# Twelve units in the row rings of two graph convolutions, and twelve early tiles of x1, in a graph network kernel on one core

## What is computed

```python
h = jnp.maximum(_layernorm(x, axis=-1), 0.0)
x = x + _L0_gnn_ref(h, src, dst, ...)          # attention, 8 heads; the sum is called x1
h = jnp.maximum(_layernorm(x, axis=-1), 0.0)
x = x + _L1_gnn_ref(h, edge_index, W1, b1, W2, b2)

def _gcn_layer(x, W, b, src, dst, n_nodes):    # twice, each with a relu behind it
    h = x @ W
    deg = segment_sum(ones, dst) + 2.0
    dinv = rsqrt(deg)
    msgs = h[src] * (dinv[src] * dinv[dst])[:, None]
    return segment_sum(msgs, dst) + h * (2.0 * dinv * dinv)[:, None] + b
```

## Time and profile before

| | us |
|---|---|
| median of three runs | 5014.36 |
| the profiled execution, as timed | 5055.62 |
| its span, first to last instruction | 5053.7 |
| TensorE matmul busy | 3857.4 (76%) |
| GpSimd busy | 2442.9 (48%) |
| VectorE busy | 2345.6 (46%) |
| ScalarE busy | 2192.1 (43%) |
| DMA | 803.60 MB, mean 159 GB/s |

### The profile page before, as it was taken

The page is one execution under the profiler, slowest core; times in us unless marked ns, Lnnn a source line. Parts: engine busy times, 40 slices in busy tenths (PEclk is TensorE's granted clock), DMA queues, the critical chain, the costliest instruction groups (busy, mean ns, idle before and its releaser), DMA issues.

```text
span 5053.7 us, 77590 instructions
## 1 busy us (share of the span) xinstructions
PE 3857.4 (76%) x18550; PEld 2260.5 (45%) x18551; DVE 2345.6 (46%) x4398; ACT 2192.1 (43%) x5340; POOL 2442.9 (48%) x2548
## 2 busy tenths in 40 slices
PE   4579998666777677779777777778897777777777
PEld 3369983455555555554323323333343333233333
DVE  5268887456666566678322222222353222222226
ACT  3245541344444444445444444444443444444444
POOL 3510001455555555543466666666503666666666
PEclk8789999788888888889888888899898888888899
DMA  6522225555555555555566665566514666656668
GB/s 246 156 56 59 82 62 167 159 154 160 157 163 156 143 149 149 147 150 199 182 177 174 176 177 169 167 174 176 159 68 147 180 176 179 172 166 170 174 173 309
DMA packets 317266, 803.60 MB, mean 159 GB/s; under 512 B 67665, under 2 KB 97251, under 8 KB 316241
## 3 DMA queue, kind: packets, MB, share of 16 engines
q0 software_dynamic: 193760, 629.95, 43.6%
q1 hardware_dynamic: 94981, 120.30, 7.5%
q10 hardware_dynamic: 28428, 52.40, 3.0%
HBM read 718.21 MB, written 85.04 MB: 159 GB/s over the span
## 4 chain that ended last, share of the span: by engine, by line
PE 56%; another core or an unknown queue 18%; issue 11%; ACT 6%; DVE 4%; ACTq 2%; DMA 1%; SPq 1%; DVEq 1%; POOL 0%; POOLq 0%
PE mm L1661 13%; PE tr L1661 12%; PE mm L1490 7%; PE mm L1582 4%; PE mm L1638 4%; PE tr L1582 4%; PE sm L1638 4%; ACT eler_hots L1391 3%; ACT eler_hots L1382 2%; PE tr L1638 2%; PE hist_ps L1638 2%; PE sm L1527 1%; PE tr L1485 1%; DVE big L854 1%
## 5 line engine op out<-in xcount | busy, mean ns | idle before, releaser
L1249 POOL DMA_INDIRECT edge<-h_tab,src_group x1564 | 1493.6, 955 | 1098.5 <-issue 425.2
L1391 ACT ACTIVATE eler_hots<-eler_hots,ones 128x256 f32<-128x256 f32 x1320 | 663.6, 503 | 1192.6 <-remote 632.0
L1661 PE MATMUL tr<-edge,eler_hots 128*128 x1760 | 932.6, 673 | 304.9 <-DVE big L854 130.5
L1661 PE MATMUL mm<-edge,eler_hots 128*128 x1760 | 918.4, 667 | 290.1 <-ACT eler_hots L1391 173.2
L1249 POOL DMA_INDIRECT rows_wmat<-v_tab,src_group x782 | 741.3, 948 | 601.2 <-DVE edge L828 363.0
L1382 ACT ACTIVATE eler_hots<-iota,ndrel 128x128 f32<-128x128 f32 x2640 | 915.9, 394 | 178.6 <-issue 15.6
L1661 PEld LDWEIGHTS mm<-edge,eler_hots 128*128 128x128 f32 x1760 | 371.0, 216 | 823.5 <-issue 817.5
L854 DVE TENSOR_TENSOR big<-big,mm 128x512 f32 x440 | 302.6, 688 | 935.5 <-remote 391.3
L1661 PEld LDWEIGHTS tr<-edge,eler_hots 128*128 128x128 f32 x1760 | 365.0, 213 | 828.1 <-issue 828.0
L854 DVE TENSOR_TENSOR big<-big,tr 128x512 f32 x440 | 302.6, 688 | 806.4 <-remote 334.9
L1638 PE MATMUL mm<-edge,eler_hots 128*128 128x260 f32 x1176 | 419.5, 442 | 272.8 <-ACT eler_hots L1391 176.1
(11 more groups left out here) (231 smaller groups left out, 3897.2 us busy)
## 6 DMA issues: line engine op xcount, KB each, us to landing
h_tab<-rows_wmat SPq DMA_DIRECT2D x98, 256.0 KB, 2.0
edge<-h_tab,src_group POOLq DMA_INDIRECT x1564
rows_wmat<-low_tab SPq DMA_DIRECT2D x191, 128.0 KB
ht_tab<-rows_wmat SPq DMA_DIRECT2D x49, 256.0 KB
big<-ht_tab ACTq DMA_DIRECT2D x49, 256.0 KB
v_tab<-rows_wmat ACTq DMA_DIRECT2D x49, 256.0 KB
x_tab<-big SPq DMA_DIRECT2D x49, 256.0 KB, 2.1
rows_wmat<-v_tab,src_group POOLq DMA_INDIRECT x782
```

The lines of the kernel that those rows point to most:

```text
L1249: pool.indirect_dma_start(ring[:, 2 * u + c, :], None, tab, bass.IndirectOffsetOnAxis(ap=src_group[:, n:n + 1], axis=0)).then_inc(a["rows_ ...
L1391: act.activation(onehot[:, s.j % 2, :, :], dist[:, :, :], ACT.Relu, bias=ones[:, 0:1], scale=-1.0).then_inc(a["onehot_set"], 1)
L1661: last = pe.matmul(sum_ps[bank][:, :], onehot[:, s.j % 2, n, :], edge[:, ds(slot[0][s.j] + n * D, D)], start=(n == 0), stop=(n == 1))
```

## The change

The ring of the graph convolutions has 12 units, 24 slots, and takes nearly all of `edge`. The eight tiles of x1 that lay behind the ring have no place there; EARLY_X1 is 12, all in the row and weight buffers, loaded where twelve were loaded before. ScalarE's loads behind the stores so are 37, not 29, and each is issued 12 tiles and not 20 ahead of its tile. 12 is no power of two, so the slot of a step is computed in the way of the ring of 6.

```diff
-RING = (6, 8)
-SIXTH = -(-2 ** 16 // 6)
+RING = (6, 12)
+PARTS = [-(-2 ** 16 // units) for units in RING]
...
-EARLY_X1 = 20
+EARLY_X1 = 12
...
-        early_x1 = edge[:, 2 * RING[1] * D:2 * RING[1] * D + 8 * D].rearrange("p (s n) -> p s n", n=D)
...
-            return early_x1[:, t, :] if t < 8 else rows[:, t - 8, :] if t < 16 else wmat[:, t - 16, 0:D]
+            return rows[:, t, :] if t < SLOTS else wmat[:, t - SLOTS, 0:D]
...
-            did(dve.tensor_scalar(slotcol_i[0][:, :], gidx[:, :], float(SIXTH), None, ALU.mult))
-            did(dve.tensor_scalar(slotcol_i[0][:, :], slotcol_i[0][:, :], 16, None, ALU.arith_shift_right))
-            did(dve.tensor_copy(cols[:, 4, :], slotcol_i[0][:, :]))
-            did(dve.scalar_tensor_tensor(cols[:, 5, :], cols[:, 4, :], -float(RING[0]), cols[:, 0, :], ALU.mult, ALU.add))
-            did(dve.tensor_scalar(slotcol_i[0][:, :], cols[:, 5, :], -1.0, float(2 * AW), ALU.add, ALU.mult))
-            did(dve.tensor_scalar(slotcol_i[1][:, :], gidx[:, :], RING[1] - 1, None, ALU.bitwise_and))
-            did(dve.tensor_scalar(slotcol_i[1][:, :], slotcol_i[1][:, :], float(2 * D), None, ALU.mult))
+            for slotcol, units, part, width in zip(slotcol_i, RING, PARTS, (AW, D)):
+                did(dve.tensor_scalar(slotcol[:, :], gidx[:, :], float(part), None, ALU.mult))
+                did(dve.tensor_scalar(slotcol[:, :], slotcol[:, :], 16, None, ALU.arith_shift_right))
+                did(dve.tensor_copy(cols[:, 4, :], slotcol[:, :]))
+                did(dve.scalar_tensor_tensor(cols[:, 5, :], cols[:, 4, :], -float(units), cols[:, 0, :], ALU.mult, ALU.add))
+                did(dve.tensor_scalar(slotcol[:, :], cols[:, 5, :], -1.0, float(2 * width), ALU.add, ALU.mult))
...
             sp.wait_ge(agg[1]["step_sum"], SP)
-            for t in range(8):
-                sp.dma_start(x1_buffer(t), x1_tab[t * P:(t + 1) * P, :]).then_inc(x1_early_in, 16)
-
...
             sp.wait_ge(b_added, TILES)
-            for t in range(8, EARLY_X1):
+            for t in range(EARLY_X1):
                 sp.dma_start(x1_buffer(t), x1_tab[t * P:(t + 1) * P, :]).then_inc(x1_early_in, 16)
```

## The result

The changed kernel takes 5039.5 us (median of six runs) against 5010.5 us of the kernel before in the same comparison; the measured ratio is 1.0042, with a 95% interval of 1.0023 to 1.0061. It is not the quotient of the two medians, which is 1.0058. Put on the median of 5014, the ratio is +21 us (+12 to +31); the medians are 29 us apart; the forecast was +10. Slower, and in the range, but for the size the forecast sits just under the interval.

A forecast was written before the change was run, and what follows sets the result against it. Late-finishing matmul steps, not missing rows, were taken to bound the convolutions. Fills +3 and +5, x1 in the tail +2 and slot numbers +0.5 sum to +10.5, say +10, on 5014: 5024 us, range 4930 to 5060.

The forecast's parts named there:

- Held steps: Convolutions: matmul steps finishing late although rows have landed; VectorE waits 382.6 us in 69 waits, 5.5 us each.
- Ring, steady part, 0: Convolutions after the first fill: 12 units leave the same cycle of six or seven steps, so 0 us.
- Ring, first fill, +3 and +5: Opening of each convolution: longer ring fills later, 8 us lost, partly regained; net +3 and +5 us.
- Given back at the end: Behind GpSimd's last gather: four units more run unheld, regaining 5 us in the first convolution, 3 in the second.
- Last gather 7 us further ahead of the end: Sign that the forecast is right: GpSimd's last gather some 7 us further ahead of the stage's end.
- How a held step ends: Convolutions: over 3.5 to 4.8 us after the last gather starts, or after 7 to 9 us if gathers never pause.
- x1 in the tail, +2: Tail of the second convolution: eight more x1 loads, with less lead, cost +2 us (0 to +5).
- The eight loads left out behind the first convolution: Stage behind the first convolution: TensorE hides these x1 loads, so their absence gives 0 us (0 to -1).
- Slot numbers: VectorE, ahead of the table of slots: division takes five small instructions, not two, +0.5 us (0 to +1).
- A: Convolutions: the hold comes once in a turn of the ring; -73 us each, 4868 us; chance 0.26.
- B: Second convolution's tail, steps 406 to 439: DMA queues set the pace, +18 us, 5040 us; chance 0.12.
- C: Convolutions: holds have nothing to do with gathers, so the ring changes nothing; 5016 us; chance 0.07.

The follow-up runs named there:

- both capped kernels: Changed kernel, GpSimd's lead at each convolution's start capped at 8 units for 24 units, or at 4 plus one per 8 gathered: 5034.3 and 5038.68 us.
- the repeat: The changed kernel as it is, measured again beside the kernel before: 5090.05 us against 5073.53 us, ratio 1.002 (1.000 to 1.004).
- x1_lead3: Changed kernel with 8 early tiles of x1, not 12, on a chip without held steps: 4187.3 us, ratio 1.0003 to the kernel before.

## Why the prediction was right, and where it wasn't

**What bounds the kernel: right.** Held steps set the pace, not rows: with plain loads in place of gathers a convolution falls from 1181 to 755 us from first to last sum.

**Ring, steady part, 0: right within what can be read.** Steps 100 to 400 take 779 to 793 us with 12 units and 792 to 799 with 8; on one chip in one comparison 792 / 793 against 794 / 799, a gain of 3 and 6 us at most. Held steps in the first convolution: 63 and 67 with 12 units, 69 and 74 with 8, 58 with 6.

**Ring, first fill, +3 and +5: the formula right, the net a little small.** The first standstill came at gathers = 2 x (12 + steps done), 36 gathers and six steps, 43.9 us after the first gather; forecast 2511, which is 47 us after 2464. The working has a slip there: 23 gathers less 6.9 are 16 at 2484, not 17, and the same formula then gives 2513. It came sooner because the held steps were longer than the 8 us assumed, six steps done and not seven or eight. Eight sums and not eleven at 51 us. The gross loss, 8 us for each convolution, measured 5 to 9 in the first and 9 to 17 in the second at step 100. Given back at the end: 5 forecast and 5 to 8 measured in the first; 3 forecast and 0 to 1 in the second. That last term is the one mis-sized. Last gather 7 us further ahead of the end: 8.5 us. What was wrong is the name. The loss isn't bound to the opening: both capped kernels have it too, at 1.0023 and 1.0027.

**How a held step ends: wrong.** I took it that a pause of GpSimd ends it, 3.5 to 4.8 us after the last gather starts, and 7 to 9 us without one. At the opening of the changed kernel the hold ended 6.0 us after the last gather's start (2513.37 to 2519.41), and in the repeat 7.0 us after it. With gathers 1.45 us apart 84 held steps ended within 4.5 us and GpSimd had not paused. Nothing in the sum hung on it but the 8 us per held step of the first fill, which the trace had shown directly, and the 3.5 us to land. That the total came near all the same is partly luck: the sum of the first fill rests on this picture of a pause.

**x1 in the tail, +2: not contradicted, but too small to be seen.** Rings of 8 with the late x1 are at 1.0004, 2 us (-9 to +13). In the changed kernel's tail VectorE's addition of x1 never waited for a DMA (0.4 us in all, on another cause). The eight loads left out behind the first convolution show nowhere: 196 us and 197 us. Slot numbers: the first gather of the attention stage starts at 903 to 911 us in the kernels on holding chips, before at 909; +0.5 can't be seen.

**The rivals.** A is out: 63 held steps against 69, not 40, rings of 6 as fast as 8, and holds at the same steps with rings of 6, 8 and 12. B is out at a lead of seven steps on the holding chips. C, that held steps have nothing to do with the gathers, is out by the plain loads; the pauses that I held against it were weak evidence, but the conclusion was right. The rule of the Trainium skill cited there ("SBUF — State Buffer", section "SBUF: two separate sides"), that DMA can't slow compute in SBUF, agrees with the plain loads (268 and 294 GB/s, TensorE's steps in 755 and 768 us). What was drawn from it, that gathers don't hold matmuls, the measurement decides against. Whether the holds have to do with SBUF at all no run shows.

**The size.** +10 against +21 (+12 to +31) in the first comparison and +10 (0 to +20) in the second; by the medians +29 and +16.5. So in the first comparison it is too small, by a factor of two to three. The two intervals overlap at 1.0023 to 1.004. From the table, rings of 12 against 8 in one comparison are -2 in the first convolution and +10 in the second; the runs' medians say 5090 - 5076 = +14. One execution each can't settle where the rest lies.

**Open.** What a held step is. It comes with indirect gathers, and not on every chip. Nor is it settled that the matmuls are what is late. At the first hold of the kernel before, TensorE had been handed all entries of two steps:

```profile
2483.06 3.69 PE L1661 MATMUL mm<-edge,eler_hots 128*128 x8
```

By this row they are done at 2486.75, but the two sums start at 2492.67 and 2500.38. The ends of matmuls are modelled, so either the matmuls ran on or their completion was signalled late; where this text says that TensorE is held, it means either. Besides, a convolution took 1180 to 1207 us with rings of 6 to 12, with the start capped or not, at 1.25, 1.305 and 1.45 us a gather, though held steps were 58 or 84 and 2.9 or 5.8 us long. That looks as if something held the average, and no run here tested that.

## What to carry to other kernels

A longer ring helps only where the consumer ever lacks rows; look at the consumer's waits first. Here the producer's standing still was an echo of the consumer's holds, and four more units in stock only cost the time to put them there. Pull the suspected cause out whole (plain loads in place of gathers, 426 us a stage) ahead of tuning around it, and take a gain or loss of 0.2% for what it is: this one is smaller than the difference between two profiles of the same kernel.

## What the runs showed of the hardware

- The same kernel (before) took 4187 us on one chip and 5010 to 5074 us on the others, 17% less. Most of the difference is held steps: x1_lead3, traced there, has one gap over 4.5 us, and takes 983 us in the attention stage and 985 and 1001 us in the convolutions, where holding chips take 1325 to 1379 and 1180 to 1207 with rings of 6 to 12. Its granted clock is 0.99 in these stages, not 0.84 to 0.93.
- The holds come with indirect gathers issued by GpSimd, not with plain loads: 268 GB/s from SyncE's queue and 294 GB/s from GpSimd's own held nothing.
- In one stretch of the convolutions ten given steps were held in 9 to 13 of 16 stages, with rings of 6, 8 and 12.
- GpSimd is busy for 0.54 us with a plain load of 128 rows, and for 0.95 with a gather of as many.
- A gather issued 1.45 us after the one before makes held steps shorter (2.9 us on average against 5.8) and more (84 against 67), and the stage no shorter (1190 us). At 1.305 us nothing changes.
